# Query, key and value projections as seven block products of half-sized operands, with the weight blocks fetched piece by piece by SyncE's queue

## The reference, cut to what matters

```python
h = layernorm(x)
q = relu(h @ Wq + bq); k = relu(h @ Wk + bk); v = relu(h @ Wv + bv)      # 512 x 512 weights
e = q @ k.T / sqrt(512) - 10000 * causal
y = softmax(e) @ v
x = x + layernorm(relu(y @ Wo + bo))
x = x + layernorm(ffn(layernorm(x)))     # gated sparse feed-forward, not touched by the change
```

## Time and profile before

| | |
|---|---|
| median of 3 runs | 2062.92 us (2062.69 to 2063.83) |
| the profiled execution | 2062.52 us, span 2060.4 us |
| PE busy | 2002.2 us, 97% |
| DVE busy | 1520.3 us, 74% |
| ACT, POOL busy | 1101.9 us, 1108.7 us |
| DMA | 194.85 MB, 95 GB/s on average |
| granted TensorE clock | 0.998 |

### The profile page before, as it was taken

One profiled execution on the slowest core, in us unless ns is written; L12 is line 12 of the kernel. 1 busy time (PEld: TensorE's weight loads), 2 busy tenths in 40 slices (PEclk: granted clock), 3 DMA queues, 4 the chain that ended last, 5 costly groups with the idle time before them and its releaser, 6 DMA issues. The chain is left out here.

```text
span 2060.4 us, 30926 instructions
## 1 busy us (share of the span) xinstructions
PE 2002.2 (97%) x9419; PEld 937.9 (46%) x9419; DVE 1520.3 (74%) x3285; ACT 1101.9 (53%) x2268; POOL 1108.7 (54%) x1304
## 2 busy tenths in 40 slices
PE   8999999999999999999999999998999999999997
PEld 4444444444444444444444444453444444444443
DVE  6576554677555467565547765579999999999999
ACT  5444433344333434443334443335888888888885
POOL 2243322354323245333225432325999999999997
PEclk9999999999999999999999999999999999999999
DMA  5234342344342334423343332261222223223221
GB/s 185 75 92 112 73 99 73 99 110 110 86 102 76 78 90 125 102 77 95 78 94 97 110 88 66 88 179 63 80 96 93 88 87 98 94 96 97 89 78 67
DMA packets 301593, 194.85 MB, mean 95 GB/s; under 512 B 223858, under 2 KB 241394, under 8 KB 301428
## 3 DMA queue, kind: packets, MB, share of 16 engines
q1 hardware_dynamic: 301428, 192.88, 33.7%
HBM read 82.69 MB, written 58.72 MB: 69 GB/s over the span
## 5 line engine op out<-in xcount | busy, mean ns | idle before, releaser
L631 PE MATMUL psum<-hT,w_hi 128*128 128x512 f16 (+1 forms) x1544 | 458.3, 379 | 0.0
L631 PE MATMUL psum<-kT,qT 128*128 128x512 f16 (+3 forms) x1920 | 363.4, 347 | 1.5 <-DVE kT L1173 1.5
L631 PE MATMUL psum<-v,pT 128*128 128x512 f16 x1632 | 362.5, 379 | 0.7 <-DMA pT<-phl 0.7
L631 PE MATMUL psum<-hT,w_lo 128*128 128x512 f16 (+1 forms) x772 | 292.3, 379 | 0.0
L631 PEld LDWEIGHTS psum<-kT,qT 128*128 128x128 f16 x1920 | 180.9, 98 | 184.1 <-issue 2.9
L905 ACT ACTIVATE sS<-sS,nm 128x128 f32<-128x128 f32 (+7 forms) x64 | 76.9, 1201 | 345.9 <-DVE nm L1216 345.8
L894 ACT ACTIVATE raw<-psum,bqkv_s 128x512 f32<-128x512 f32 x192 | 131.2, 683 | 218.7 <-PE psum L631 216.5
L631 PEld LDWEIGHTS psum<-v,pT 128*128 128x128 f16 x1632 | 159.7, 98 | 193.1 <-issue 1.2
L1528 DVE MAX8 c<-cut 128x8 f32<-128x512 f32 x384 | 247.0, 691 | 0.0
L631 PEld LDWEIGHTS psum<-hT,w_hi 128*128 128x128 f16 x1544 | 151.5, 98 | 176.2 <-DVE w_lo L1147 0.3
L1655 POOL TENSOR_SCALAR ve<-mv 128x1 f32<-128x1 f32 x64 | 22.5, 352 | 348.2 <-DVE mv L1242 347.3
(11 more groups left out here) (177 smaller groups left out, 3754.2 us busy)
## 6 DMA issues: line engine op xcount, KB each, us to landing
xg<-x SPq DMA_DIRECT2D x64, 256.0 KB, 5.1
xr<-x SPq DMA_DIRECT2D x64, 256.0 KB, 2.9
h_scratch<-hb SPq DMA_DIRECT2D x64, 256.0 KB, 3.0
h<-h_scratch SPq DMA_DIRECT2D x64, 256.0 KB, 2.7
x<-x_scratch SPq DMA_DIRECT2D x64, 256.0 KB, 3.0
x_scratch<-xr SPq DMA_DIRECT2D x62, 256.0 KB, 2.0
out<-zn SPq DMA_DIRECT2D x59, 256.0 KB, 2.0
xcg<-xc_scratch SPq DMA_DIRECT2D x16, 512.0 KB, 4.1
```

Of the source, the lines that this page charges most:

```text
L631: mm = nc.tensor.matmul(outp, stat(a), mov(c), start=(n == 0 and k == 0), stop=(n == total - 1 and k == 2))
```

## The change

For groups 1 to 15 each projection is made from seven products of blocks instead of eight (a 2 x 2 x 2 split of contraction, outputs and tokens, each half being 256). Each product is 2 x 2 blocks of 128 rows x three f16 terms, so 12 matmuls of 256 columns; products 0 to 3 run in the projection's first half step, 4 to 6 in its second. Group 0 keeps the plain projection. What comes with it:

- The seven weight blocks of a projection, some of them differences or sums of blocks of W, are made once at the start (`mix` on GpSimd, `mixed_hi`, `mixed_lo`), written to DRAM (`store_mixed`, 42 DMAs) and read back into a single buffer `ring` of 7 x 256 KB. SyncE's `refill` fetches the blocks for the next projection into it in four pieces (products 0-1, 2-3, 4-5 of 512 KB each, and 6 of 256 KB) once TensorE has finished with the old ones. Pieces 0 and 1 are issued in half steps 1, 3, 5, behind `rows_of` and, in half step 1, behind `transpose_p`; pieces 2 and 3 in half steps 2, 4, 6.
- h needs seven blocks too: four `difference` and seven `lo_h` on GpSimd (four `lo_h` before), seven `hi_h` on ScalarE (four before), 14 DMA transposes a group (8 before).
- The products' results are combined: `copy` on ScalarE reads PSUM into `part` (two instructions of 256 columns, four copies a projection), the sums are `sum_quarter` on VectorE; `hi_quarter` (ScalarE) and `lo_quarter` (VectorE) make the f16 pair, four each. Some products accumulate in a bank that a copy must have read before, and PSUM's six banks are split, three for projections and `values`, three for scores.
- On VectorE `ln_stats` of tiles 0 and 1 moves from half step 7 to half step 0, behind the convolution. `load_x` moves from half step 5 to the end of 7.

The core of the diff:

```diff
-                    for j in range(GROUP):
-                        pe.wait_ge(hT_in[j].sem, hT_in[j].at(g - 1))
+                def products(kind, g, part_of):
+                    def multiply(p, first):
+                        h = hT_early[:, g % 2, p] if p < 4 else hT_late[:, p - 4]
+                        for m in range(2):
+                            for c in range(2):
+                                for n, (a, b) in enumerate(((0, 0), (0, 1), (1, 0))):
+                                    mm = nc.tensor.matmul(P_BANKS[p][:, 256 * m:256 * (m + 1)], ring[:, p, a, c, P * m:P * (m + 1)],
+                                                          h[:, b, c, :], start=(first and m + c + n == 0), stop=(c == 1 and n == 2),
+                                                          skip_group_check=True)
+                        mm.then_inc(vqk_ps.sem, 1)
+                    def arrived(n):
+                        pe.wait_ge(w_in[n], 16 * (run + 2))
+                        pe.wait_ge(hT_in[n].sem, hT_in[n].at(g - 1))
+                    if part_of == 0:
+                        arrived(0)
+                        vacated(0, (vqk_ev, COPY_U3), (vqk_lo, SUM_22))
+                        multiply(0, True)
+                        vacated(1, (vqk_lo, SUM_12))
+                        multiply(1, True)
+                        arrived(1)
+                        vacated(2, (vqk_lo, SUM_21))
+                        multiply(2, True)
+                        pe.wait_ge(vqk_ev.sem, vqk_ev.at(step_at(kind, g, COPY_1)))
+                        multiply(3, False)
...
+                def refill(kind, g, *pairs):
+                    run = run_of(kind, g) + 1
+                    for n in pairs:
+                        if run < len(VQK) * (NG - 1):
+                            a, b = ((0, 2), (2, 4), (4, 6), (6, 7))[n]
+                            sp.wait_ge(vqk_ps.sem, vqk_ps.at(product_at(kind, g, b - 1)))
+                            sp.dma_start(ring[:, a:b].rearrange("p q a c n -> p q (a c n)"), wc_d[run % len(VQK), :, a:b, :]) \
+                                .then_inc(w_in[n], 16)
...
                     rows_of(H)
                     if h == 1 and pv_tile(H) is not None:
                         transpose_p(GROUP * (g - 1) + 1)
+                    if 0 < g < NG and h < 6 and h % 2:
+                        refill(VQK[h // 2], g, 0, 1)
+                    if 0 < g < NG and h in (2, 4, 6):
+                        refill(VQK[h // 2 - 1], g, 2, 3)
...
 ScalarE
                     elif h == 1:
                         early = s_tile(H - 1)
-                        if st:
-                            relu(*st[0])
+                        if kind:
+                            hi_12(kind, g)
+                            copy_u3(kind, g)
+                        hi_p(early, first)
...
 VectorE
                         late(H, (3, convolution))
                     elif h == 1:
-                                lo_vqk(*st[n])
+                        if kind:
+                            sum_12(kind, g)
+                            sum_22(kind, g)
+                        lo_p(early, first)
+                        if kind:
+                            lo_12(kind, g)
+                            sum_21(kind, g)
+                        lo_p(early, rest_of)
...
+                    if g + 1 < NG:
+                        if h == 0:
+                            ln_stats(g + 1, 0)
+                            ln_stats(g + 1, 1)
```

More of the change, by code:

```diff
@@ L82, in stages @@
     kind, c = (VQK + ("vo",))[h // 2], 2 * (h % 2)
-    return [(kind, g, c), (kind, g, c + 1)] if g < NG else []
+    if g >= NG:
+        return []
+    if g and kind != "vo":
+        return [("products", kind, g, h % 2)]
+    return [(kind, g, c), (kind, g, c + 1)]
 def s_tile(H):
@@ new lines, in _ @@
+                        hi_p(early, first)
+                        if kind:
+                            hi_22(kind, g)
+                            hi_21(kind, g)
+                        hi_p(early, rest_of)
+                    elif h in (2, 4):
+                        if kind:
+                            copy_1(kind, g)
+                        exponential(s)
+                        if kind:
+                            copy_5(kind, g)
+                        hi_p(s, first)
+                        if kind:
+                            hi_11(kind, g)
+                            copy_u2(kind, g)
+                        hi_p(s, rest_of)
+                    elif h in (3, 5):
+                        if kind:
+                            hi_12(kind, g)
+                            copy_u3(kind, g)
+                            hi_22(kind, g)
+                            hi_21(kind, g)
+                    elif h == 7:
+                        exponential(s)
+                        for n, span in ((0, first), (1, rest_of)):
+                            hi_vo(*st[n][1:])
+                            hi_p(s, span)
@@ L981, in _ @@
                         normed(due(H, 1))
-                    if h == 3 and g + 1 < NG:
-                        for j in range(GROUP):
-                            hi_h(g + 1, j)
+                    if 3 <= h < 7 and g + 1 < NG:
+                        hi_h(g + 1, *((0, 2), (1,), (3,), (4, 5, 6))[h - 3])
                     if due(H, 4) == 0:
@@ L1357, in _ @@
                     s, st = s_tile(H), stages(H)
-                    if h == 0:
-                        if st:
-                            lo_vqk(*st[0])
+                    kind = VQK[h // 2] if h < 6 and 0 < g < NG else None
+                    if g == 0 and h < 6:
+                        for i in st:
+                            lo_vqk(*i)
+                    elif h == 0:
+                        if kind:
+                            sum_11(kind, g)
                         late(H, (2, residual_stats))
-                        if st:
-                            lo_vqk(*st[1])
-                        if s is not None:
-                            score_rows(s)
+                        if kind:
+                            lo_11(kind, g)
+                        score_rows(s)
                         late(H, (3, convolution))
@@ L1368, in _ @@
                         early = s_tile(H - 1)
-                        for n, part in ((0, first), (1, rest_of)):
-                            if st:
-                                lo_vqk(*st[n])
-                            if early is not None:
-                                lo_p(early, part)
-                        late(H, (3, convolution))
-                        if g + 1 < NG:
+                        if kind:
+                            sum_12(kind, g)
+                            sum_22(kind, g)
```

468 lines of the change are left out of this document (317 added, 151 removed).

## The result

The changed kernel takes 2343.95 us (median of 4 runs, 2343.44 to 2347.4) against 2063.38 for the kernel before on the same chip: ratio 1.1363, 95% interval 1.1344 to 1.1383, 281 us slower. The forecast was 2157 us, 2080 to 2195. The direction was right, the size was not, and the time lies outside the range.

A forecast was written before the change was run, and what follows sets the result against it. TensorE, busy 97% of the span, was taken to bound the kernel. The terms -53.5 + 121 + 5 + 22 - 3 + 3 = +94.5 us on 2062.5 us gave 2157 us, range 2080 to 2195.

The forecast's parts named there:

- TensorE's stream: Projections of groups 1 to 15: 84 matmuls of 256 columns replace 48 of 512, 1.19 us less each, together -53.5 us.
- product 0 of q waits for the ring: Start of q in groups 1 to 15: TensorE waits for a refill issued late behind transpose_p, +121 us.
- the other refills: Pieces 0 and 1 for k, issued in half step 3: 1.2 us of waiting in four one-chunk groups, +5 us.
- `values` waits for VectorE: First values in one-chunk groups: needs k's sum_22 after 9.2 to 9.5 us against 3.93; 5.5 us each, +22 us.
- granted clock: Rival: a half-speed stretch of 3.4 us follows each of 15 waits, +25 us; with late copies 2192 us; chance 0.12.
- copies before product 3: Within the clock rival: ScalarE's first copy of k comes late, 2.6 us in four groups, +10 us.
- group 0 and the start of g = 1: Three mixes, 42 stores and 1.8 MB read back, with group 0's 43 us as cover: +3 us.
- What the refill meets in half step 1: q's first refill follows transpose_p, which awaits lo_p, made 4.1 us later; landing takes 4.1 us more; waits +121 us.
- The second piece: Refill for products 2 and 3 lands 3.4 to 3.7 us behind the first, against 2.62 needed: 0.8 us each time.
- Groups of four chunks: Three groups with attention over four chunks: q waits 5.2 us at the ring, plus 0.8, 16 us in sum.
- that weights come in time: Rival: refills arrive in time and TensorE stays the bound, 2009 us, or 2031 with the wait before values; chance 0.15.
- The wash with half the `values` wait: Rival: no 4.1 us shift and 3 us landing, 2080 us; with half that wait, within 0.2% of before; chance 0.07.

The follow-up runs named there:

- the best, at 2194 us: Refill first in half step 1, store_xc one half step earlier, VectorE's sums ahead of the convolution, against the changed kernel with two copies per transpose: 2194.17 us, ratio 1.0631.
- three copies: Changed kernel with each of its 530 DMA transposes replaced by three plain copies: 2515.64 us, ratio 1.2181.
- both edits: Refill first in half step 1 and store_xc one half step earlier, against the changed kernel with two copies per transpose: 2196.4 us, ratio 1.0636.

## Why the prediction was wrong

In us, each term of the sum against the changed kernel:

| term | forecast | measured |
|---|---|---|
| TensorE's stream | -53.5 | -53.4 |
| product 0 of q waits for the ring | +121 | +152.6 |
| the other refills | +5 | +5.1 |
| `values` waits for VectorE | +22 | +30.1 |
| idle time that the kernel before has | -3 | -2.3 |
| granted clock | 0, 25 as a rival | +57.9 |
| copies before product 3 | 0, 10 in that rival | +24.4 |
| score banks | 0 | +19.7 |
| last transposes of h before product 6 of v ("issue") | 0 | +15.5 |
| group 0 and the start of g = 1 | +3 | +20.7 |

The changed kernel's waits in this table make 268.1 us, beside 275.8 us of new gaps; the rest is spread over small waits.

- **TensorE's gain** was right to 0.1 us. 256-column matmuls cost 109.2 ns each here too, where the clock is full. PE busy did not fall by the forecast's 50 us but rose from 2002.2 to 2017.2: the lower clock took the gain back.
- **The step that failed** is "What the refill meets in half step 1". Its chain from `ln_stats` to `lo_p` is right, and so is the landing of the first piece. It took VectorE to arrive at that chain as in the kernel before; instead VectorE came 8.0 us later in g = 5, held by the store, and the transposes went out at 17.5 us where it had 11.8. The forecast had counted what VectorE's new order adds, but of SyncE's new order only what stands right ahead of the refill; of the four loads of x, moved from half step 5 to the end of 7, and the transposes of the last block of h, it never asked what is behind them. The store of the channel rows is, and VectorE's convolution waits for it. Shown by the store moved (-90 us, the refill back at the forecast's times), by the loads moved (wait of 106 us down to 39), and by g = 15. This step is worth 90 of the 187 us that the forecast was short; the other half are terms that it put at nothing or too low, the clock above all.
- **The second piece** was given 0.8 us of waiting each time, from 1024 KB in 7.8 us. It lands 1.2 to 1.5 us behind the first, inside the 2.62 us of products 0 and 1, and nothing waited for it there: 12 of the 121 us never came.
- **Groups of four chunks** did not wait at the ring, for which the forecast had 5.2 us: the late VectorE made TensorE wait 5.6 to 6.5 us for a score bank there, and the refill arrived meanwhile. The lost time stands under another name; with the store moved, 0.9 to 1.9 us turn up at the ring.
- **The clock** was a rival at +25 us and 0.12. It should have been in the sum: the forecast had 15 waits of 5 to 13 us, and its own row showed the fall after a much shorter one. I had halved one stretch of 3.4 us for each of 15 waits; there were 28 stretches, at 2.1 us each on average. In the experiments this term shrinks with the gaps (280.8 and 57.9; 196.4 and 56.4; 147.4 and 41.8), but it wasn't isolated.
- **`values`**: four waits of 7.2 to 7.6 us in groups of one chunk, forecast 5.5 (its own terms add up to 9.1 us and not 9.2 to 9.5, so 5.2). The place and mechanism are those of the forecast; reordering VectorE takes them away, with no gain in time.
- **Group 0**: no wait of TensorE before 90 us is for a DMA, so the 42 stores that were feared cost nothing that the trace shows. Two of the waits (7.7 and 7.5 us) come from `mixed_hi` and its partners: in the trace ScalarE idles 10.35 us for GpSimd's mix of weights, with the reads of q's PSUM banks queued behind, and PSUM has three banks for them instead of six. That is read from the trace, no run isolates it.
- **Copies and the transposes of h**: the copy before product 3 costs 2.6 to 2.8 us in seven groups, each time in v; at k, where the forecast had looked for it, 0.9 to 1.3 us in three. That product 6 of v would wait for the last transposes of h was nowhere in the forecast.
- **The rivals**: that weights come in time had its conditions stated at 8 us sooner, and even with the refill put first other waits took over; 53 us of waits in total was never near. The wash with half the `values` wait would have been 2069.5 us, 0.34% above the kernel before and not within 0.2%. The range's upper end had clock and copies together at 35 us; they came to 82, on top of the store.

Undoing the two mistakes of order recovers 147 of 280 us. No version here beats the kernel before; the best, at 2194 us, still loses some 147 us in gaps and 40 to the clock against a gain of 53.

## What to carry to other kernels

When an issue is moved in a queue that serves several engines, list what now stands behind it and who waits for that, not only what stands ahead of the new work; a store that lets a buffer be written again is as much a dependency as a load. A saving on the engine that bounds the kernel is safe only as long as it stays fed: at 97% busy, each new wait is paid in full, and a long one in part again in the clock (281 us of gaps here, and 58 us of slower matmuls). And when an edit takes a wait away, look for the same us under another name (bank, part, copies) before counting them as gained.

## What the hardware showed

- Two plain copies within SBUF hold SyncE for 1.29 us and one transposing DMA for about 1.27, both for 128 rows of 512 f16; three copies hold it 1.93 us. An engine whose queue seemed idle enough turned 350 us more of issue into 172 us.
- The first refill of 512 KB in half step 1 lands in 3.9 to 4.4 us in the changed kernel, the second, issued 0.6 us later, in 4.7 to 5.1; in the kernel with both edits, where in nearly all groups four loads of x and a store go out just ahead, the first takes 4.7 to 7.2. The small store of channel rows (128 KB) goes from 2.0 us to 3.8 to 5.8 behind the four loads of x.
- 81 MB of refills, in a kernel that moves 126 GB/s on average, made 4.6 us of difference by themselves (14 at most), where VectorE ended the waits at q in either case.
- A wait that the trace names "issue" was one for a DMA: 11 times in the changed kernel and 17 times with three copies, TensorE started 0.1 us after the last rows of h had landed.
